# Attention weights turned by two engines: ten key tiles by VectorE and the exchange, three by PE

## What is computed

```python
C_q = Q @ Wq_d                      # 4 x 512 x 128
C_kv = K @ Wkv_d                    # 4 x 1601 x 64
CqWqk = (C_q @ W_qk).reshape(b, n, H, LKV)      # H = 16, LKV = 64
scores = jnp.einsum('bnhl,bkl->bhnk', CqWqk, C_kv) / sqrt(LKV)
attn = jax.nn.softmax(scores, axis=-1)
V_up = (C_kv @ Wv_u).reshape(b, nkv, H, HD)     # HD = 64
out = jnp.einsum('bhnk,bkhd->bnhd', attn, V_up)
```

## Time and profile before

| | us |
|---|---|
| median of 3 runs | 3124.07 (3120.61 to 3132.83) |
| the profiled execution | 3122.95 |
| its span, first to last instruction | 3121.1 |
| PE matmul busy in the span | 2634.9 (84%) |
| DVE busy | 2387.7 (77%) |
| ACT busy | 1363.6 (44%) |
| POOL busy | 1947.4 (62%) |
| mean granted PE clock | 0.937 |

### The profile page before, as it was taken

The page is one execution under the profiler, slowest core; times in us unless marked ns, Lnnn a source line. Parts: engine busy times, 40 slices in busy tenths (PEclk is TensorE's granted clock), DMA queues, the critical chain, the costliest instruction groups (busy, mean ns, idle before and its releaser), DMA issues. The chain is left out here.

```text
span 3121.1 us, 38588 instructions
## 1 busy us (share of the span) xinstructions
PE 2634.9 (84%) x13600; PEld 1977.1 (63%) x13600; DVE 2387.7 (77%) x2167; ACT 1363.6 (44%) x2095; POOL 1947.4 (62%) x1303
## 2 busy tenths in 40 slices
PE   6786867787777877787778599999999699999997
PEld 3554645555545555565555378888887578888886
DVE  1526666777777967797778569999999689999998
ACT  2242633444343533444344354554544445454453
POOL 1000356654666466655666388888887488888884
PEclk8888989999998988898899799999999899999998
DMA  7305599977898799878897612222221322222221
GB/s 242 133 3 185 189 268 255 259 180 180 247 253 223 205 255 250 252 198 227 254 258 195 189 49 79 71 75 73 69 75 61 135 72 71 75 69 81 68 75 68
DMA packets 176290, 481.26 MB, mean 154 GB/s; under 512 B 36065, under 2 KB 55394, under 8 KB 176098
## 3 DMA queue, kind: packets, MB, share of 16 engines
q1 hardware_dynamic: 171234, 468.77, 51.7%
q10 hardware_dynamic: 4864, 10.03, 0.9%
HBM read 244.24 MB, written 70.85 MB: 101 GB/s over the span
## 5 line engine op out<-in xcount | busy, mean ns | idle before, releaser
L937 ACT ACTIVATE b_pr<-b_sc,b_nm 128x799 f32<-128x799 f32 (+1 forms) x512 | 473.2, 929 | 750.5 <-DVE b_nm L998 749.7
L887 PE MATMUL b_po<-b_pt,shared 128*64 128x256 f32 x3328 | 505.8, 427 | 234.6 <-POOL b_pt L1097 115.3
L998 DVE TENSOR_REDUCE b_nm<-b_sc 128x1 f32<-128x1604 f32 x256 | 467.4, 1826 | 242.9 <-PE b_sc L873 242.2
L1378 DVE SCALAR_TENSOR_TENSOR c_acc<-c_ps,c_sd,c_acc 128x1024 f32<-128x1024 f32 x448 | 572.5, 1282 | 92.5 <-PE c_ps L1276 92.5
L1320 ACT ACTIVATE c_scaled<-c_ps,c_sgu 128x1024 f32<-128x1024 f32 x336 | 375.3, 1117 | 446.7 <-PE c_ps L1276 438.9
L1097 POOL COPY b_pt<-b_tn 32x832 f32<-32x832 f32 x512 | 448.7, 876 | 193.4 <-DVE b_tn L1004 169.4
L1004 DVE STREAM_TRANSPOSE b_tn<-b_pr 128x1664 f32<-128x1664 f32 x256 | 487.7, 1905 | 69.8 <-POOL b_pt L1097 57.1
L887 PEld LDWEIGHTS b_po<-b_pt,shared 128*64 128x64 f32 x3328 | 270.5, 149 | 417.5 <-issue 281.1
L873 PE MATMUL b_sc<-b_kh,b_qs 128*128 128x402 f32 (+1 forms) x1024 | 410.8, 401 | 70.0 <-ACT b_pr L937 65.8
L1431 POOL TENSOR_TENSOR c_sum_u<-c_sum_u,c_scaled 128x1024 f32<-128x1024 f32 x168 | 404.8, 2410 | 76.0 <-ACT c_scaled L1320 74.9
L1431 POOL TENSOR_TENSOR c_sum_g<-c_sum_g,c_scaled 128x1024 f32<-128x1024 f32 x168 | 404.9, 2410 | 67.9 <-ACT c_scaled L1320 67.3
(11 more groups left out here) (175 smaller groups left out, 3499.3 us busy)
## 6 DMA issues: line engine op xcount, KB each, us to landing
b_pt<-b_tn SPq DMA_DIRECT2D x1536, 104.0 KB, 3.8
c_uw_int<-wint_u SPq DMA_DIRECT2D x56, 512.0 KB, 3.4
c_gw_int<-wint_g SPq DMA_DIRECT2D x56, 512.0 KB, 3.4
c_dw_int<-wint_d SPq DMA_DIRECT2D x56, 512.0 KB, 3.4
a_cx<-in_b_ctxT SPq DMA_DIRECT2D x16, 1608.0 KB, 10.8
b_rw<-in_c_gw SPq DMA_DIRECT2D x28, 512.0 KB, 4.8
b_rz<-in_c_gz SPq DMA_DIRECT2D x28, 512.0 KB, 6.3
wint_g<-b_rw SPq DMA_DIRECT2D x28, 512.0 KB, 3.0
```

Source lines behind the costliest of these rows:

```text
L887: ins = T.matmul(po[z * LAT:(z + 1) * LAT, s * 256:(s + 1) * 256], cn[:, b, t, :], pt[s][:, :, :, 32 * t:32 * t + 32].rearrange("p a z e - ...
L937: S.activation(pr[u % 2][:, k0:k1], sc[:, at + lo:at + hi], ACT.Exp, bias=nm[:, u % 2:u % 2 + 1], accum_out=den[:, g % 2, q, half:half + 1 ...
L998: V.tensor_reduce(nm[:, u % 2:u % 2 + 1], both, AXY, ALU.max, negate=True).then_inc(s_nm, 1)
L1378: V.scalar_tensor_tensor(out=total, in0=pair[SLOT[x, j] % 4][:, :], scalar=scale(x, j), in1=total, op0=ALU.mult, op1=ALU.add).then_inc(s_a ...
```

## The change

The order in which keys stand in `b_tn` is altered, and with it the split of the turning.

- `NDT` = 10: DVE turns the first ten key tiles (1280 keys) as before, so its instruction reads 1280 columns instead of 1664, and a block to be placed has 640 elements a row instead of 832.
- The last three tiles are turned by PE (`turn` in `tensor`, three transposes by the identity, into the bank `b_mi`) for every unit, and ACT copies them to `b_pe` (`keep_turned`), which has three buffers, one per pair. `b_mi` now has a user in every step. In steps where it is used by an output, a projection or a latent turn (`special`), the turn stands behind the first half of the next unit's scores, otherwise ahead of it.
- The 16 blocks of a pair: nine by DMA (`BY_DMA`), six by POOL (`BY_POOL`: the four that stay on their partitions and two that don't), one by ACT (`BY_SCALAR`, `cross`, a copy across partitions).
- On DVE the output and the latent copy come ahead of the transposition of the same step.
- Where latent keys are turned (in the mixer too), tiles 10 to 12 take one matmul each instead of four.

```diff
+NDT = 10
+SEG = 32 * NDT
-def key_tile(kv, t, c):
-    return kv[0:LAT, c * (KPAD // 4) + 32 * t:c * (KPAD // 4) + 32 * t + 32]
+def key_tiles(kv, t):
+    if t >= NDT:
+        return [(slice(0, P), kv[0:LAT, t * P:(t + 1) * P])]
+    return [(slice(32 * c, 32 * c + 32), kv[0:LAT, c * SEG + 32 * t:c * SEG + 32 * t + 32]) for c in range(4)]
...
+BY_POOL = [(0, 0), (1, 1), (2, 2), (3, 3), (0, 1), (2, 3)]
+BY_SCALAR = [(3, 2)]
+BY_DMA = [(0, 2), (1, 3), (2, 0), (3, 1), (1, 2), (3, 0), (0, 3), (1, 0), (2, 1)]
...
+def special(k):
+    return k in CN_AT or k % 8 == 5 and k + 3 < NU or k % 4 == OUT_AT % 4 and k >= OUT_AT
...
         def moved(eng, p):
-            eng.wait_ge(s_move[p % 2], 12 * 16 * (p // 2 + 1))
-            eng.wait_ge(s_diag, 4 * p + 4)
+            eng.wait_ge(s_move[p % 2], len(BY_DMA) * 16 * (p // 2 + 1))
+            eng.wait_ge(s_block, len(BY_POOL) * (p + 1))
+            eng.wait_ge(s_cross, len(BY_SCALAR) * (p + 1))
...
                 if part == 0:
                     moved(T, p)
+                    T.wait_ge(s_pe, 2 * p + 2)
...
+                    if t < NDT:
+                        turned = pt[s][:, :, :, 32 * t:32 * t + 32].rearrange("p a z e -> p z a e")
+                    else:
+                        turned = pe[p % 3][:, t - NDT, :, :]
...
+            def turn(u):
+                ev = ("turn", u, 0)
+                bank_free(T, ev)
+                T.wait_ge(s_ex, 2 * u + 2)
+                for t in range(NDT, NKT):
+                    ins = T.transpose(mi[:, (t - NDT) * P:(t - NDT + 1) * P], pr[u % 2][:, t * P:(t + 1) * P], ident[:, :])
+                ins.then_inc(s_tr, 1)
...
+                if 1 <= k <= NU and not special(k):
+                    turn(k - 1)
                 if k + 1 < NU:
                     scores(k + 1, 0)
+                if 1 <= k <= NU and special(k):
+                    turn(k - 1)
...
+            def keep_turned(u):
+                S.wait_ge(s_tr, u + 1)
+                if u >= 6 and u % 2 == 0:
+                    S.wait_ge(s_pv, u // 2 - 2)
+                S.copy(pe[u // 2 % 3][:, :, u % 2, :], mi[:, 0:(NKT - NDT) * P].rearrange("p (t e) -> p t e", e=P)).then_inc(s_pe, 1)
+
+            def cross(p):
+                s = p % 2
+                S.wait_ge(s_tt, 2 * p + 2)
+                if p >= 2:
+                    S.wait_ge(s_pv, p - 1)
+                for a, c in BY_SCALAR:
+                    S.copy(pt[s][32 * c:32 * c + 32, a, :, :], tn[s][32 * a:32 * a + 32, c, :, :]).then_inc(s_cross, 1)
...
-                V.transpose(tn[u // 2 % 2][:, :, u % 2, :], pr[u % 2][:, :].rearrange("p (c e) -> p c e", c=4)).then_inc(s_tt, 1)
+                V.transpose(tn[u // 2 % 2][:, :, u % 2, :], pr[u % 2][:, 0:4 * SEG].rearrange("p (c e) -> p c e", c=4)).then_inc(s_tt, 1)
...
-                for a in range(4):
-                    at = slice(32 * a, 32 * a + 32)
-                    G.tensor_copy(pt[s][at, a, :, :], tn[s][at, a, :, :]).then_inc(s_diag, 1)
+                for n, (a, c) in enumerate(BY_POOL):
+                    G.tensor_copy(pt[s][32 * c:32 * c + 32, a, :, :], tn[s][32 * a:32 * a + 32, c, :, :]).then_inc(s_block, 1)
```

More of the change, by code:

```diff
@@ L328, in turn_keys @@
                     at = (t - CN_TURNS[k][0]) * LAT
-                    for c in range(4):
-                        ins = T.matmul(ps[7][32 * c:32 * c + 32, at:at + LAT], key_tile(keys["kv"], t, c), ident[0:LAT, 0:LAT],
-                                       start=True, stop=True)
+                    for rows, tile in key_tiles(keys["kv"], t):
+                        ins = T.matmul(ps[7][rows, at:at + LAT], tile, ident[0:LAT, 0:LAT], start=True, stop=True)
                 ins.then_inc(s_cnp, 1)
@@ L690, in ring_events @@
             out.append(("cn", *CN_AT[k]))
-    return out
+        if 1 <= k <= NU:
+            out.append(("turn", k - 1, 0))
+    return out
+def special(k):
+    return k in CN_AT or k % 8 == 5 and k + 3 < NU or k % 4 == OUT_AT % 4 and k >= OUT_AT
 def attention(nc, d, kvd, cq, ident, shared, raw, wint, x1, x2):
@@ L725, in attention @@
         pt = [sb(f"b_pt{j}", [P, 4, 2, SEG]) for j in range(2)]
+        pe = [sb(f"b_pe{j}", [P, NKT - NDT, 2, P]) for j in range(3)]
         ot = sb("b_ot", [P, NB])
@@ L758, in bank_free @@
                     eng.wait_ge(s_ql, g + 2)
+                elif kind == "turn":
+                    eng.wait_ge(s_pe, g + 1)
                 elif kind == "cn":
@@ L843, in turn_latent @@
                     at = (t - chunk[0]) * LAT
-                    for c in range(4):
-                        ins = T.matmul(mi[32 * c:32 * c + 32, at:at + LAT], key_tile(kv, t, c), ident[0:LAT, 0:LAT],
-                                       start=True, stop=True)
+                    for rows, tile in key_tiles(kv, t):
+                        ins = T.matmul(mi[rows, at:at + LAT], tile, ident[0:LAT, 0:LAT], start=True, stop=True)
                 ins.then_inc(s_cnp, 1)
@@ L957, in scalar @@
                     out_latent(k // 4 - 2)
+                if 1 <= k <= NU and not special(k):
+                    keep_turned(k - 1)
                 if k < NU:
                     exponent(k, 0)
+                if 1 <= k <= NU and special(k):
+                    keep_turned(k - 1)
+                if k % 2 and 3 <= k < 2 * PAIRS + 3:
+                    cross((k - 3) // 2)
                 if k >= 64 and k % 64 == LN_VAR + 2:
@@ L1088, in split_keys, with blocks @@
                 G.tensor_tensor(kl[b % 2][:, 0:NKV], kv[:, 0:NKV], kh[b % 2][:, 0:NKV].bitcast(F32), ALU.subtract).then_inc(s_kl, 1)
-            def diagonal(p):
+            def blocks(p):
                 s = p % 2
@@ L1130, in gpsimd @@
                 if p < PAIRS:
-                    diagonal(p)
+                    blocks(p)
                 if p % 2 and p < PAIRS:
```

21 lines of the change are left out of this document (9 added, 12 removed).

## The result

The changed kernel takes 3069.92 us, the median of 4 runs (3068.14 to 3074.18), against 3124.59 for the kernel before (4 runs, 3120.61 to 3132.83; 3124.07 was the median of the first three). The ratio is 0.9824, with an interval from 0.9801 to 0.9846. That is 54.7 us gained, where 21 were forecast, and it lies outside the range. The profiled execution took 3070.59 (span 3068.8), 52.3 less of span than before.

What follows compares the result with a forecast made beforehand. It took working pairs as bound by store, loads, landing and POOL, quiet steps by maximum, exponential and scores. Terms +1.2 - 7.6 + 3 - 14 - 3.6 = -21 on 3122.95 gave 3102 us, range 3075 to 3130.

Steps and rivals of the forecast that it cites:

- The bound: Attention's working pairs, which also prepare FFN weights: a closed loop of store, loads, landing, 3.5 us of POOL, next store.
- Working pairs: 0: Attention pairs that also prepare FFN weights: 0 per pair, between -0.1 and +0.1 us; two key splits add +1.2 us.
- the loads land sooner: Rival for working pairs: a smaller exchange frees bandwidth for the loads, -59 us, total 3042; chance 0.08.
- Batch starts: -7.6: Start of each batch: first store waits for SP, the last exchange ahead takes 1.9 us less, four batches, -7.6 us.
- Quiet steps: +3: Attention steps without FFN weight preparation: output steps 0.4 us longer, projection steps 0.44 shorter, ordinary ones unchanged; +3 us in all.
- Quiet waits: -14: Attention stretches without FFN weight preparation: PE's waits for exchange DMAs shrink, -14 us, between -8 and -20.
- Tail: -3.6: End of attention: SP is free sooner, so PE's last weighing starts sooner; -3.6 us.
- Rest: 0: Fewer matmuls for three key tiles and VectorE's output ahead of its transposition: 0 us in all; FFN not touched.
- become the bound: Rival for quiet steps: PE's transposes and bank waits cost 1.17 us per unit, +52 us, total 3154; chance 0.12.
- Nothing is gained: Rival for starts, waits and tail: these stay, as nine exchanges take as long as twelve; +4 us, total 3127; chance 0.18.

Runs made afterwards that it cites:

- the swap of two calls: On SP a block's loads issued ahead of the store of the block before: 2971.25 us in the kernel after, 3058.33 us in the kernel before.
- the split alone: Kernel after, but all 13 key tiles turned by VectorE and none by PE; nine DMAs, six POOL copies, one ACT copy kept: 3096.7 us, ratio 0.9893.
- the turn alone: Kernel after with three tiles still turned by PE, but twelve DMAs of 80 KB, four POOL copies, none by ACT: 3088.08 us, ratio 0.9863.

## Why the prediction was wrong, point by point

**The bound: right.** Store, loads, landing, POOL, store is the loop. The kernel after shows it in the same rows, and the swap of two calls moved it by 7.5% and 10.8%.

**Working pairs: 0. This is the step that failed.** It measured -40.8 us over 80 intervals, -0.51 per pair, against bounds of 0.1 either way. Its reasons on POOL and SP held: nine DMAs and six copies, all hidden. A copy of before and one of after:

```profile
L1097 POOL COPY b_pt<-b_tn x512: 867/876/888, 405.0 to 1740.9; 32x832 f32<-32x832 f32 x171
L1147 POOL COPY b_pt<-b_tn x768: 706/713/724, 404.2 to 1681.6; 32x640 f32<-32x640 f32 x192
```

The copy gets shorter with its length, but less than in proportion: 0.88 us for 832 elements and 0.71 for 640, where 0.67 would be. The prediction's 0.92 had the pauses between copies in it. With them six take 4.60 us, 0.9 more than the four and not 0.6. Crossing partitions costs nothing here (minimum 706, maximum 724 ns, with both kinds among them). SP's slack grew from 1.72 to 2.91, not to 3.6, since the loop got shorter and the exchange starts later in it. What failed was to say that the landing, 7.47 us of the loop, was a constant. I held that the exchange couldn't touch loads issued before it. The trace of before spoke against that, and I read it the other way. I took the landing times of the whole exchange, 2.1 to 8.1, as those of transfers that wait their turn behind three others, without looking at single ones. The records of before hold the answer. The twelve DMAs of a pair share one semaphore, and each adds 16 to it, in single steps as its parts land. The first is issued 0.89 us after the zero-point load (medians of 83 pairs). When the load has landed, the semaphore has risen by 30 in the median, by at least one in 82 of the 83 pairs and by 92 at most; its sixteenth step comes 0.43 us *ahead* of the landing. The steps don't tell which DMA they are of, so a whole one need not have landed; but transfers that wait until the loads are through could show no step at all.

The Trainium skill, "DMA: Bandwidth & Descriptors", section on queues, rings and completion order, says that an engine takes a ring's descriptors in ring order, and in the same place that completion isn't first in, first out for the engine that issues; I drew from the first half alone that a smaller exchange can't help the loads. The measurement decides against what I drew, for the whole transfer: 7.75 us became 7.23 and 6.62 with less behind it, and 6.83 with nothing. The rule for a single ring is neither borne out nor refuted by it. Whether an engine keeps the order within itself, while the sixteen run apart from each other so that one is at the exchange while another still has load packets, I haven't shown; steps of the exchange's semaphore ahead of the load's landing would fit it.

The rival "the loads land sooner" had the mechanism, with 0.7 us per pair where 0.51 was measured, and -59 where the loop gave -40.8. It stood at 0.08 because I let the order of issue outweigh a DMA share of 0.89.

**Batch starts: -7.6.** Measured -9.6, and -9.3 with the split alone: right. The store at 729.69 still goes at the end of SP's long run of DMAs.

**Quiet steps: +3.** The turn alone made the quiet part 3.5 longer; the ordinary step, that with an output and that with a projection measured 4.05, 4.45 and 4.85 against 4.05, 4.49 and 4.80. PE's turn and ACT's copies, timeline and lines of the kernel after:

```profile
1302.21 1.94 PE L905 MATMUL b_po<-b_pt,shared 128*64 128x256 f32 x14
1304.09 0.55 PE L915 MATMUL b_mi<-ident,b_pr 128*128 128x128 f32 x3
1304.39 0.43 PE L886 MATMUL b_sc<-b_kh,b_qs 128*128 128x402 f32 x1
```

```profile
L983 ACT COPY b_pt<-b_tn x128: 720/721/724, 409.6 to 1677.8; 32x640 f32<-32x640 f32 x128
L975 ACT COPY b_pe<-b_mi x256: 468/480/493, 399.4 to 1677.3; 128x384 f32<-128x384 f32 x128
```

The records of successive products overlap, so the price is read from start to start, as the prediction read the output's: 1304.39 - 1304.09 = 0.30 us behind a weighing, and 0.25 where the turn stands behind scores (1314.02 to 1314.27), with 0.4 taken; ACT's copies 0.48 and 0.72 with 0.45 and 0.7 taken. The Trainium skill, "TensorEngine Tiling (Array Packing)", key properties, has TensorE drain where the tiling mode changes. No second drain shows: the turn here stands between the 64-wide weighing and the 128-wide scores and takes 0.05 us more than behind scores, and the step with an output grew from 4.14 (maxima at 1361.70 and 1365.84 before) to 4.45, by less than the 0.4 that I added.

**Quiet waits: -14.** With the +3 above the quiet part was to fall by 11, and fell by 9.9. Without the 3.5 of the turn alone that is -13.4, within the bounds; the split alone gave -6.9, just outside them. The waits of rows 6 are all but gone, 1.5 us of 26.0.

**Tail: -3.6.** Measured -1.6. The last weighing (from 1686.43) no longer waits for its exchange, as forecast, but PE isn't through with the pair before it, whose weighing still waits. Before and after:

```profile
1741.59 3.67 PE L887 MATMUL b_po<-b_pt,shared 128*64 128x256 f32 x14 [4.93 <-DMA b_pt<-b_tn]
```

```profile
1679.48 2.51 PE L905 MATMUL b_po<-b_pt,shared 128*64 128x256 f32 x14 [2.77 <-DMA b_pt<-b_tn]
...
1686.43 2.88 PE L905 MATMUL b_po<-b_pt,shared 128*64 128x256 f32 x20
```

That wait ends 9.4 us behind the last maximum before and 7.7 after, which is the gain. From its end to the FFN both kernels take the same, 33.2 and 33.3 us, so the 1.05 us that the last weighing waited before brought nothing more. PE's granted clock was lower there, 0.72 (1682 to 1692) against 0.90 before (1744 to 1754); that this took the rest back isn't tested. The term came to less than half its size.

**Rest: 0.** The FFN, whose code is the same, took 9.6 us longer in this execution. Stretches of it with the busy time of PE, PEld, VectorE, ACT and POOL and their counts, the granted clock, DMA share and GB/s, after:

```profile
1702.00:1712.00 10.00, 0.00 (x0) 0.00 (x0) 0.00 (x0) 0.00 (x0) 0.00 (x0) 0.50 0.79 279
...
1772.00:1782.00 10.00, 8.39 (x24) 6.67 (x25) 5.77 (x6) 1.49 (x3) 7.64 (x4) 0.66 0.06 15
...
2388.00:2538.00 150.00, 131.87 (x559) 107.81 (x560) 110.53 (x94) 73.37 (x76) 116.39 (x49) 0.91 0.26 87
```

and the same parts before:

```profile
1834.00:1844.00 10.00, 8.17 (x36) 6.81 (x37) 8.34 (x8) 3.60 (x4) 9.84 (x5) 1.00 0.16 52
...
2450.00:2600.00 150.00, 135.05 (x591) 110.10 (x590) 118.47 (x100) 76.62 (x78) 124.23 (x52) 0.96 0.24 81
```

With PE idle at the stage's start its clock is at the lower level, 0.50 or 1.2 GHz, in both. At 1772 us it fell again from 1.00 to 0.66 of full speed (a mean between 2.4 GHz and 1.2) where the same stretch of before had 1.00, and 24 matmuls were done in 10 us instead of 36; PE had been busy 8.0 of the 10 us ahead of it after, 8.3 before. In the longer stretch the clock was 0.91 against 0.96, with 559 matmuls against 591. In the other executions the same FFN took 1346.4 to 1352.9 us, 1350.6 in the kernel after when it was run again. What sets the clock at these places, and whether the change has a part in it, is open. The attention alone gave 61.9 us (58.0 by the second trace of the kernel after).

**The other rivals.** PE did not become the bound, at 0.30 us for three transposes where this rival had 0.93. "Nothing is gained" fell with the starts and the waits, which the split alone shows.

## What to carry to other kernels

Where a stage's period holds a transfer's landing time, price that landing as something that other traffic stretches, behind it as well as ahead of it: here 0.5 us of 7.75 went when the exchanges around the loads shrank from 1248 to 720 KB, and 0.9 when there was none behind them. Then look at what order alone puts into the loop: a queue that waits for a store before it issues the next load made a loop out of two things that need not wait for each other, and swapping them was worth 94 us, more than the change. And cut two traces at the same events, not at round times, before saying which term was wrong.

## What the hardware showed

An exchange DMA of 32 partitions costs SP 0.62 us to issue at 13 KB (7.48 for twelve) as at 104 (7.52), so splitting work over fewer DMAs pays on SP and making them smaller pays in the landing of others. Three fp32 transposes of 128x128 take PE 0.25 to 0.30 us from their start to that of the next product, and PE's clock stays at 1.00 of full speed in the quiet stretches that have them in every step. A 32x640 copy costs 0.71 us on POOL, across partitions or not, and 0.72 on ACT, across partitions.
